# Adaptive-norm layers, one core: the last tile's norm moved from the end of the experts into the first turn of the linear attention

## The reference

```
h = _layernorm(x) * (1 + ca) + sa
x = x + ga * _L0_attn_ref(h, ...)      # causal linear attention, 16 heads
h = _layernorm(x) * (1 + cb) + sb
x = x + gb * _L0_ffn_ref(h, ...)       # 64 experts, routed by groups of 64 tokens
h = _layernorm(x) * (1 + ca) + sa      # the second layer's own ca, sa
x = x + ga * _L1_attn_ref(h, ...)      # linear attention over a whole batch
h = _layernorm(x) * (1 + cb) + sb
x = x + gb * _L1_ffn_ref(h, ...)       # FP4-quantised gated network
```

```
kv = jnp.einsum('bnd,bne->bde', k, v)
z = 1.0 / (jnp.einsum('bnd,bd->bn', q, k.sum(axis=1)) + EPS)
attn = jnp.einsum('bnd,bde,bn->bne', q, kv, z)
```

## Time and profile before

| what | value |
|---|---|
| median of 3 runs | 925.78 us (923.56 to 929.38) |
| the profiled execution | 928.15 us |
| its span, first to last instruction | 926.4 us |
| TensorE busy | 780.6 us (84%) |
| VectorE busy | 704.0 us (76%) |
| ScalarE busy | 457.5 us (49%) |
| GpSimd busy | 231.4 us (25%) |
| mean granted TensorE clock | 0.934 of 2.4 GHz |

### The profile page before, as it was taken

How to read it: one execution, slowest core, us unless ns; L and a number is a source line. 1 busy time by engine, 2 the same in 40 slices (tenths; PEclk the granted TensorE clock), 3 DMA queues, 4 the chain that set the end, 5 groups by cost and what they waited for, 6 DMA issues and landing times. The chain is left out here.

```text
span 926.4 us, 26347 instructions
## 1 busy us (share of the span) xinstructions
PE 780.6 (84%) x10674; PEld 444.1 (48%) x10674; DVE 704.0 (76%) x1336; ACT 457.5 (49%) x796; POOL 231.4 (25%) x194
## 2 busy tenths in 40 slices
PE   7398999989887846889997988989999688768986
PEld 3276766766666612333443433333343266435552
DVE  4455546889999869999978776788888545659994
ACT  5355666666565514656786861211111235457762
POOL 6560101001000120000006574333333100007661
PEclk9689999999998967999998988999999889889997
DMA  7200000000000002656676668787888100000000
GB/s 244 96 4 4 5 4 5 5 4 5 4 5 4 4 0 92 238 237 251 269 243 250 250 249 312 255 269 253 260 277 280 55 2 1 0 1 9 26 24 34
DMA packets 33890, 104.89 MB, mean 113 GB/s; under 512 B 4400, under 2 KB 6256, under 8 KB 33264
## 3 DMA queue, kind: packets, MB, share of 16 engines
q1 hardware_dynamic: 33200, 102.28, 31.0%
q10 hardware_dynamic: 576, 0.99, 0.3%
HBM read 53.98 MB, written 48.23 MB: 110 GB/s over the span
## 5 line engine op out<-in xcount | busy, mean ns | idle before, releaser
L1291 PE MATMUL bank<-RS,Wd 128*128 128x512 f32 x256 | 134.1, 613 | 9.4 <-DVE RS L1354 9.3
L1354 DVE TENSOR_TENSOR RS<-so_ug,bank 128x512 f32<-128x512 f32 x128 | 84.2, 673 | 25.1 <-PE bank L1277 12.8
L958 ACT ACTIVATE att_qk<-bank 128x512 f32<-128x512 f32 x128 | 66.7, 602 | 57.4 <-PE bank L728 57.4
L1256 POOL TENSOR_TENSOR so_ug<-so_ug 128x512 f32<-128x512 f32 x48 | 63.6, 1326 | 110.7 <-DMA so_ug<-hidden 110.7
L1291 PEld LDWEIGHTS bank<-RS,Wd 128*128 128x128 f32 x256 | 48.1, 195 | 60.5 <-issue 29.7
L1597 POOL TENSOR_TENSOR so_made<-so_ug 128x512 f32<-128x512 f32 x23 | 35.6, 1563 | 159.9 <-DVE bank L1800 149.3
L1621 ACT ACTIVATE so_ug<-bank,bu 128x512 f32<-128x512 f32 x80 | 54.7, 683 | 18.2 <-PE bank L57 18.1
L55 PE MATMUL bank<-Hhi,Wgh 128*128 128x512 f16 x128 | 50.0, 391 | 8.5 <-DVE so_made L1752 8.4
L1052 DVE TENSOR_TENSOR att_am<-bank,causal 128x512 f32<-128x512 f32 x32 | 22.0, 688 | 43.1 <-PE bank L765 43.0
L460 DVE TENSOR_TENSOR att_sorting<-att_sorting 128x256 f32<-128x256 f32 x103 | 49.8, 484 | 0.0
L55 PE MATMUL bank<-Hhi,Wuh 128*128 128x512 f16 x128 | 49.8, 389 | 0.0
(11 more groups left out here) (415 smaller groups left out, 1900.1 us busy)
## 6 DMA issues: line engine op xcount, KB each, us to landing
so_ug<-hidden SPq DMA_DIRECT2D x48, 768.0 KB, 4.8
hidden<-so_off SPq DMA_DIRECT2D x48, 512.0 KB, 3.0
hidden<-so_made SPq DMA_DIRECT2D x80, 256.0 KB, 2.0
so_ug<-hidden SPq DMA_DIRECT2D x16, 512.0 KB, 4.4
XT<-in_L_attn_x_dram SPq DMA_DIRECT2D x8, 256.0 KB, 7.0
out_dram<-ff_xo SPq DMA_DIRECT2D x8, 256.0 KB, 2.0
keys<-in_L_ffn_Wup_dram SPq DMA_DIRECT2D x1, 1024.0 KB, 4.9
F<-in_L_ffn_Wgate_dram SPq DMA_DIRECT2D x1, 1024.0 KB, 7.2
```

Of the source, the lines that this page charges most:

```text
L958: nc.scalar.activation(qk[t % 2][:, r, :, :].rearrange("p a l -> p (a l)"), psF[r], ACT.Relu).then_inc(s_["fe"], 1)
L1256: nc.gpsimd.tensor_tensor(u, u, g, ALU.mult).then_inc(s_pp, 1)
L1291: nc.tensor.matmul(psY[j][:, :], Wd[:, n, :], hh[n % 4][:], start=False, stop=n == EBLK - 1).then_inc(s_dn[n % 4], 1)
L1354: nc.vector.tensor_tensor(hh[i][:], pg[four % 2][:, i if four % 2 else i // 2 * 3 + i % 2, :], psW[k % 4][:, :], ALU.mult).then_inc(s_hh[k ...
```

## The change

The nine steps behind the experts' last tile are deleted. In the last layer nine semaphores are added (62 in all), and the steps stand at these places of its streams: the centring product is TensorE's first instruction, ahead of the wait for `one`; the square takes the place of ScalarE's table load; the variance stands behind `keys_values(1)`, Ln and Exp behind `values(1)`, the multiplication behind `keys(1)`, scale and offset (to ot0) behind `keys(2)`, Hhi behind `values(2)`, Hlo behind `queries(1)`. `keys_values(14)` waits for Hhi and Hlo.

```diff
 # experts, TensorE / ScalarE / VectorE
                 tiles(pe, tile)
-                centre(NT - 1)
-                variance(NT - 1)
...
                 tiles(act, tile)
-                normal(NT - 1, NB - 1)
...
                 tiles(dve, tile)
-                normalise(NT - 1, NB - 1)
-                h_low(NT - 1)
 # last_layer
+                names += ("last_cen", "last_sq", "last_var", "last_ln", "last_rs", "last_xn", "last_h", "last_hi", "last_lo")
+                last = slice((NT - 1) * ST, NT * ST)
 # TensorE
                         def keys_values(g):
                             upto(pe, "k", g - 1)
+                            if g == 4 * NB - 2:
+                                upto(pe, "last_hi", 1)
+                                upto(pe, "last_lo", 1)
...
+                        def last_centre():
+                            nc.tensor.matmul(psC, centre_w[:], XT[:, last], start=True,
+                                             stop=True).then_inc(s_["last_cen"], 1)
+                        def last_variance():
+                            upto(pe, "last_sq", 1)
+                            nc.tensor.matmul(psT, mean_w[:], sq[:], start=True, stop=True).then_inc(s_["last_var"], 1)
...
                                 keys_values(4 * b + 1)
+                            if b == 0:
+                                last_variance()
...
+                        last_centre()
                         upto(pe, "one", 4)
 # ScalarE
+                        def last_square():
+                            upto(act, "last_cen", 1)
+                            nc.scalar.activation(sq[:], psC, ACT.Square).then_inc(s_["last_sq"], 1)
+                        def last_root():
+                            upto(act, "last_var", 1)
+                            nc.scalar.activation(rs[:], psT, ACT.Ln, bias=eps_ln[:]).then_inc(s_["last_ln"], 1)
+                            upto(act, "last_ln", 1)
+                            nc.scalar.activation(rs[:], rs[:], ACT.Exp, scale=-0.5).then_inc(s_["last_rs"], 1)
+                        def last_high():
+                            upto(act, "last_xn", 1)
+                            nc.scalar.activation(Hhi[:, last], xn[:], ACT.Identity, bias=mod[:, 1, 0, NB - 1:NB],
+                                                 scale=mod[:, 1, 1, NB - 1:NB]).then_inc(s_["last_hi"], 1)
...
                                 values(4 * b + 1)
+                            if b == 0:
+                                last_root()
...
                                 values(4 * b + 2)
+                            if b == 0:
+                                last_high()
...
-                        nc.scalar.preload_act_table_set("natural_log_exp_and_others")
+                        last_square()
                         upto(act, "one", 4)
 # VectorE
+                        def last_normalise():
+                            upto(dve, "last_rs", 1)
+                            nc.vector.tensor_tensor(xn[:], psC, rs[:], ALU.mult).then_inc(s_["last_xn"], 1)
+                        def last_full():
+                            upto(dve, "last_xn", 1)
+                            nc.vector.tensor_scalar(ot[0][:], xn[:], mod[:, 1, 1, NB - 1:NB], mod[:, 1, 0, NB - 1:NB],
+                                                    ALU.mult, ALU.add).then_inc(s_["last_h"], 1)
+                        def last_low():
+                            upto(dve, "last_h", 1)
+                            upto(dve, "last_hi", 1)
+                            nc.vector.tensor_tensor(Hlo[:, last], ot[0][:], Hhi[:, last],
+                                                    ALU.subtract).then_inc(s_["last_lo"], 1)
...
                                 keys(4 * b + 1)
+                            if b == 0:
+                                last_normalise()
...
                                 keys(4 * b + 2)
+                            if b == 0:
+                                last_full()
...
                                 queries(2 * b + 1)
+                            if b == 0:
+                                last_low()
```

## The result

The changed kernel takes 922.33 us (median of 19 runs, 919.42 to 927.19), the kernel before 927.73 us in the runs beside it (19 runs, 922.41 to 932.6). The ratio is 0.9938, 95% interval 0.9919 to 0.9958: faster by 0.6%, some 5.8 us. The forecast was 4.7 us. The profiled execution has a span of 920.7 us where before it was 926.4.

What follows compares the result with a forecast made beforehand. The prediction took a serial chain ending the experts, one engine at a time, to set the last layer's start. Chain -7.69, semaphores +0.2 and turn 0 +2.8 gave -4.7 us: from 925.78 to 921.1 us, range 917.5 to 925.

Steps and rivals of the forecast that it cites:

- The chain at the end: End of the experts: with the serial steps removed, the stage's last instruction ends 7.69 us earlier, all of it gained.
- Semaphores: Border to the last layer: nine more give VectorE two more to raise, 0.09 us each, costing 0.2 us.
- The table load: Start of the last layer on ScalarE: removing the load is worth nothing, since ScalarE could not start sooner anyway.
- The slower rival: Last layer's inverse roots: each of nine pays two table loads of 1.28 us, giving 939 us; chance 3%.
- The centring product at the low clock: Start of turn 0 on TensorE: it runs at 1.2 GHz, so the next matmul starts 1.72 us after it.
- the late start: Start of the last layer's stream: 0 to 0.4 us late, taken as 0; 17% jointly with longer low clock or Ln load.
- The price of turn 0: Turn 0 of the last layer: the moved steps make the sum of turn 1 start 2.8 us late.
- the 4.6 us: Turn 0 on TensorE: the clock rises to the high level about 4.6 us after the first matmul.
- a gap at Hlo other than 0.7 us: End of turn 0: sign of being wrong; Hlo should end, and the sum start, about 0.7 us after the last accumulate.
- The parts 2.1 for TensorE and 0.7 for the queues: Turn 0: lateness split into 1.0 centre plus 1.1 variance, and some 0.7 for ScalarE's and VectorE's places.
- Turn 1 and what follows keep their length: Last layer from turn 1 on: lengths unchanged, so the 2.8 us delay passes on whole.
- The sum: Whole kernel: -7.69 + 0.2 + 2.8 = -4.7 us, taken off the median 925.78 to give 921.1 us.

Runs made afterwards that it cites:

- e1: The changed kernel with the nine steps of the last tile's norm left out of the last layer too; 920.92 us, ratio to the kernel before 0.9896.
- e3: The kernel before with nine more semaphores in the last layer that nothing uses; 928.45 us (1 run).
- e2: The changed kernel with the table load put back as ScalarE's first instruction of the last layer; 921.38 us, ratio to the kernel before 0.9936.
- e12: The changed kernel with all nine steps moved out of turn 0, mostly to turn 1, and one semaphore for them; 918.62 us, ratio to the kernel before 0.9923.
- e4: The changed kernel with Hhi behind values(3), and scale and offset and Hlo in turn 1 behind keys(5); 922.68 us, ratio to the kernel before 0.9924.
- e7: The changed kernel with ten unread matmuls added on TensorE at the end of the experts; 920.93 us, ratio to the kernel before 0.9945.
- e8: The changed kernel with the nine steps out of turn 0, one semaphore for them, and ten unread matmuls ending the experts; 917.98 us, ratio to the kernel before 0.9905.
- e10: The changed kernel with the last tile's norm left out and ten unread matmuls at the end of the experts; 921.68 us (1 run).
- e11: The changed kernel, places kept, with one semaphore for the nine steps and six unread matmuls ending the experts; 921.0 us, ratio to the kernel before 0.9934.

## Why the prediction was right

- **The chain at the end, 7.69 us.** Right: it is gone whole, and e1 keeps 7.4 with the longer border taken off. But 7.69 is its length in one profile, whose variance ran at the low level; in e3 the same chain took 6.73.
- **Semaphores, 0.2 us.** Right: 0.22 in the changed kernel, 0.23 in e3 alone, and gone with one semaphore. The reason given, two more on VectorE, is shown in part only, as GpSimd has two more as well and comes to the meeting as late.
- **The table load, nothing.** Right by e2. The slower rival, reloading tables in each root, did not come: ScalarE's next load is at the network's first Silu.
- **The centring product at the low clock, 1.72 us.** Right in place and size: it took 1.99, and the first group started at 737.36, 1.8 after its start. It began 0.04 us behind the memset, and the square 0.05 behind its end, so the late start that the prediction allowed for did not come. The low level under it was in part luck:

```profile
732.00:735.60 3.60, 0.03 (x1) 0.06 (x1) 0.64 (x1) 0.00 (x0) 0.07 (x2) 1.00 0.00 0
735.70:739.00 3.30, 3.30 (x9) 1.51 (x10) 0.00 (x0) 0.65 (x2) 0.07 (x3) 0.50 0.01 2
```

  The granted clock (third from the end) was still whole through the idle time and fell only within 0.1 us of the product's start. In e12, after the same 4.52 us, it fell 0.8 us into the work.
- **The price of turn 0, 2.8 us.** The mechanism was right, its sum too large for this profile: 1.95. Two terms were mis-sized. The clock rose earlier than the 4.6 us that I had taken over from the earlier trace rows: group 1 ended 4.6 us after the memset instead of 5.1, which is 0.5 us. And the row of steps on ScalarE and VectorE overlaps where I had added durations, six times about 0.06: 0.3 us. At an equal clock the price is 2.56 (against e3), near to the 2.8. One of the prediction's signs of being wrong did come, a gap at Hlo other than 0.7 us: from the end of the last `accumulate` (745.61) to the sum (745.97) it is 0.36, where the prediction's own times give 0.75 (752.1 to 752.85). Whether the centring product at the front itself brings the rise of the clock forward stays open: of the kernels that began low and open with it, four had the rise at 2.9 to 3.5 us and e4 at 5.3; of the seven that don't, two had it at 3.2 and 3.4 us and five at 4.9 to 6.2. If it does, the 1.95 is nearer to the true price than the 2.56. The parts 2.1 for TensorE and 0.7 for the queues measure as 1.5 and 1.0.
- **Turn 1 and what follows keep their length.** Right to 0.02 us in each turn. The last stretch did differ between the two profiles, by the clock and not by the change.
- **The sum.** -7.69 + 0.2 + 2.8 = -4.7 was forecast; the profile's stretch gives -5.5, the times -5.8 (0.9938, interval 3.9 to 7.5 us). Part of the 5.5 may be the clock and not the change: with the chain at 6.7 to 7.7, 0.2 for the semaphores and the price of 2.6 at an equal clock, the change itself is worth some 3.9 to 4.9 us. That is an estimate; the timed interval holds it and the 5.5 alike. 921.1 was forecast and 922.33 measured, above it although the gain was not smaller than forecast, because the kernel before came out 2 us higher in these runs (927.73 instead of 925.78).

## What to carry to other kernels

A serial chain at the end of a stage, with nothing beside it, costs its whole length here; moved into the next stage it costs what it takes from the engine that bounds that stage, plus what stands queued behind each of its steps, so choose places behind which nothing urgent waits. Here the first turn had little idle time and took 2.6 us back at an equal clock, the second turn only 0.7. Count the semaphores too: nine more made the border 0.2 us longer. And before two profiles are compared, look at what TensorE's clock was in each: of the 5.5 us between them here, some 0.6 to 1.6 may be the clock's.

## What the runs showed of the hardware that I had not expected

The level of TensorE's clock at the start of a stage is not a function of the idle time ahead of it: after 2.9 us of it, it was high in e7 and low in e8; after 4.5 us low in the changed kernel and high in e12, where it then fell under load. It first stood high in turn 0 between 2.9 and 6.2 us after the memset where it began low, and the sum of turn 1 follows at 0.4 to 0.5 us per us (of the kernels with none of the steps in turn 0: 7.77 at 3.21 in e8, 8.49 at 4.89 before, 9.12 at 6.18 in e10). The same holds in the network's last stretch: from VectorE's addition for the sixth output to that for the eighth the profiles took 14.84 us (changed) to 16.60 (e3), of one and the same code. With the stretch ahead, where the last tile's XT ended anywhere from 726.64 (e12) to 733.90 us (e11) in spans of equal work, this goes with medians in which a change of 2 us can't be seen, while it is plain in the stretches. What moves the stretch ahead was not looked into.
